# Softmax sums of the first two sequences by TensorE instead of ScalarE's accumulator

## The chip, the core and the metric

The kernel is one program on one core of a Trainium2 chip. It uses five engines that run their own instruction streams and meet at semaphores: TensorE (PE, matrix products), VectorE (DVE), ScalarE (ACT), GpSimd (POOL) and SyncE (SP, which here only issues DMAs). The time is the device time of one execution in microseconds, as the median of several runs. Nothing else of the program's quality is looked at; the question is how many microseconds one execution takes.

## What is computed

The reference is one transformer block with adaptive layer norm, on 16 sequences of 512 tokens of width 128. For every sequence, in float32:

```
h = layernorm(x) * (1 + ca) + sa
q, k, v = h @ wq.T + bq, h @ wk.T + bk, h @ wv.T + bv      # 16 heads of width 8
scores = q k^T / sqrt(8), only |i - j| <= 32 allowed
attn = softmax(scores); x = x + ga * ((attn v) @ wo.T + bo)
h = layernorm(x) * (1 + cb) + sb
top 2 of softmax(h @ gate.T) over 8 experts; the expert input is h times the expert's weight
x = x + gb * (shared expert + the chosen experts), expert = (silu(h w1) * (h w3)) w2
```

The part that the change touches is the softmax: each row of exponentials has to be divided by its sum, before or after the product with v.

## The kernel before

The 16 sequences pass through a software pipeline. While attention runs on sequence b, the experts run on sequence b - 2 and the projections prepare sequence b + 1. Each engine's instructions are written out by hand, for sequences 0 to 4 in a function `fill()`, for 5 to 11 in `body()`, for 12 to 15 in `drain()`; there is one such set per engine, and each engine works strictly in its written order. So what a sequence costs depends on the order in which these calls stand.

Attention goes by 16 steps n per sequence, each of 32 queries for all 16 heads against 96 keys. One step is this chain:

- `scores(b, n)` on PE: four matmuls into one of two halves of the accumulator `ps_s`. It waits until the exponentials of step n - 2 have left that half.
- `maximum(b, n)` on DVE: the row maxima, negated, into `nmx`.
- `probabilities(b, n)` on ACT: four exponentials of 128 x 96 into the ring `p` (4 places), each with its sum taken into `acc` by `accum_out`.
- `turn_p(b, n)` on DVE: the step transposed in blocks of 32 into the ring `pt` (8 places).
- `values(b, kb)` on PE: the products of `pt` with the block-diagonal values `vd` into `ps_O`, for block kb of 32 keys, each group of four heads into its own 32 partitions.

The sums are used in two ways. For sequence 0, `invert_row(n)` on DVE takes reciprocals of the four sums of step n and `scale_row(n)` on POOL multiplies the exponentials by them, ahead of `turn_p(0, n)`; `scale_o(0)` then only copies `ps_O` to `o`. For every later sequence the exponentials stay as they are: `invert_sums(b)` on DVE takes all reciprocals, `turn_sums(b)` on PE transposes them, `copy_sums(b)` on ACT copies them out, `put_sums(b)` on SP writes them to DRAM, `get_sums(b)` on SP reads them back spread over partitions into `rt`, and `scale_o(b)` on DVE multiplies `ps_O` by `rt`. `attn_out(b)` on PE takes `o` from there, `residual(b)` on DVE adds it to x.

Queries and keys travel through DRAM. `high_q`/`high_k` on ACT and `low_q`/`low_k` on DVE split the projections into two parts; SP writes them out (`put_q`, `put_ql`, `put_k`, `put_kl`) and reads them back in the layout for `scores` (`load_q`, `load_k`, for each half of the sequence). `load_q(b, 0)` waits until all of q is in DRAM, `scores(b, 0)` waits until the first half of q and k has landed. The router's weights go the same way (`put_scores`, `get_scores`).

In the fill, experts do not run until sequence 2 has begun, so PE has little to do during sequences 0 and 1. `warm(count)` fills its stream with matmuls whose result nobody reads; they stand in PE's order and take time there like all others.

Of the kernel before, what the change touches and what calls it, by code (L numbers as in the profile page):

```python
# [23 lines left out]
ALU = mybir.AluOpType  # L24
# [5 lines left out]
H, DH = 16, 8  # L30
# [30 lines left out]
def build(nc, x, w13, w2, wqkv, wo, gate, bias, borow, cT, wmod, out):  # L61
    ctx = ExitStack()
    with ctx:
# [32 lines left out]
        bmask = sb("bmask", [128, HJ])  # L96
        mhalf = sb("mhalf", [128, 1])
# [103 lines left out]
        rc_d, nm_d = sem("rc_d"), sem("nm_d")  # L201
# [85 lines left out]
        def _(sp):  # L287
# [146 lines left out]
            def put_sums(b):  # L434

                sp.wait_ge(rst_cp, b)
                if b > 1:
                    sp.wait_ge(r_in, 16 * b - 16)
                for h in range(2):
                    sp.dma_start(r_scr.rearrange("g j (h n) q -> h n g j q", h=2)[h], rst[:, h]).then_inc(r_wr, 16)  # L440

            def get_sums(b):

                sp.wait_ge(r_wr, 32 * b)
                if b > 1:
                    sp.wait_ge(o_d, b)
# [18 lines left out]
            def fill():  # L465
# [26 lines left out]
                load_gb(0)  # L492
# [7 lines left out]
                load_ga(2)  # L500
# [5 lines left out]
                put_sums(1)  # L506
                load_q(2, 1, 0)
                get_sums(1)
                load_k(2, 1, 0)
                load_x(4)  # L510
                load_bias(4)
                put_q(3, 1)
# [7 lines left out]
                get_scores(1, 1)  # L520
                get_scores(1, 2)
                get_scores(1, 3)
                put_sums(2)
                load_q(3, 1, 1)
                get_sums(2)
                load_k(3, 1, 1)
                put_q(4, 0)
                load_bias(5)
                load_ga(3)
                load_x(5)  # L530
                put_ql(4, 0)
                load_gb(1)
# [6 lines left out]
                load_ga(4)  # L539
# [6 lines left out]
                load_k(4, 1, 0)  # L546
                load_bias(6)
                load_gb(2)
                get_scores(2, 3)
                put_q(5, 1)  # L550
                load_x(6)
                put_ql(5, 1)
# [124 lines left out]
        def _(pool):  # L677
# [148 lines left out]
            def scale_row(n):  # L826

                pool.wait_ge(rc_d, n + 1)
                nc.gpsimd.tensor_tensor(p[:, n % PRING], p[:, n % PRING],  # L829
                                        rs[:, n, :].unsqueeze(2).to_broadcast([128, HG, MK]), ALU.mult).then_inc(nm_d, 1)  # L830
# [5 lines left out]
            def fill():  # L836

                clear_q()
                spread_var(1, l1, ln1)
                expand_v(0, 0)  # L840
                expand_v(0, 1)
                inverse(1, l1, ln1)
                shift(1, l1, ln1)
                add_bias(0)
                scale_row(0)
                normal(1, l1, ln1)
                scale_row(1)
                scale_row(2)
                scale_row(3)
                scale_row(4)  # L850
                add_bias(1)
                scale_row(5)
                scale_row(6)
                scale_row(7)
                scale_row(8)
                scale_row(9)
                scale_row(10)
                scale_row(11)
                scale_row(12)
                scale_row(13)  # L860
                scale_row(14)
                scale_row(15)
# [4 lines left out]
                add_bias(2)  # L867
                gate_wo(0)
                gate_wo(1)
# [4 lines left out]
                expand_v(1, 0)  # L874
                expand_v(1, 1)
                scaled_low(0, 0, 0)
                spread_var(3, l1, ln1)
                inverse(3, l1, ln1)
                route_scores(0)
                route_both(0)  # L880
                route_weights(0)
                shift(3, l1, ln1)
                normal(3, l1, ln1)
                add_bias(3)
                expand_v(2, 0)
# [297 lines left out]
        def _(act):  # L1183
# [65 lines left out]
            def copy_sums(b):  # L1249

                act.wait_ge(rst_mm, b)
                if b > 1:
                    act.wait_ge(r_wr, 32 * b - 32)
# [2303 lines left out]
```

## Time and profile before

| | us |
|---|---|
| median of 3 runs | 665.83 (665.41 to 667.18) |
| profiled execution, its own time | 666.87 |
| profiled execution, span from first to last instruction | 664.9 |
| PE busy over the span | 644.2 (97%) |
| DVE busy | 587.4 (88%) |
| POOL busy | 579.5 (87%) |
| ACT busy | 557.4 (84%) |
| mean granted TensorE clock | 0.993 of full speed |

All durations come from the one profiled execution. Busy shares are averages over the whole span; the filler matmuls of `warm` count as busy PE. A row of the timeline gives the start in us from the span's beginning, the duration of the row, engine, line, operation, output and inputs, shapes and a count of merged instructions; in square brackets stands how long the engine was idle before it and what ended that. Matmul ends are modelled, so the distance between two starts is the better measure of what a matmul costs.

### The profile page before, as it was taken

How to read it: one execution, taken by the hardware profiler on the slowest of the kernel's cores; microseconds unless marked ns; L12 is line 12 of the kernel's file. 1: busy time of each engine (PE TensorE's matmuls, PEld its weight loads, DVE VectorE, ACT ScalarE, POOL GpSimd, SP SyncE). 2: the span in 40 equal slices, each digit the busy share in tenths (PEclk: the TensorE clock that was granted, in tenths of full speed). 3: DMA queues.
4: the chain of work that ended last, by engine and by line, in shares of the span. 5: the costliest groups of instructions: out<-in, count | busy, mean ns of one | idle time of the engine just before them, and what ended most of it. 6: DMA issues, size and time to landing. Idle time of an engine off the chain costs nothing. (4 is left out here: it accounts for less than half of the span.)

```text
span 664.9 us, 19607 instructions
## 1 busy us (share of the span) xinstructions
PE 644.2 (97%) x6136; PEld 563.2 (85%) x6136; DVE 587.4 (88%) x1582; ACT 557.4 (84%) x2458; POOL 579.5 (87%) x684
## 2 busy tenths in 40 slices
PE   8899989999999999999999999999999999999997
PEld 6888768888888898989898888888898888888776
DVE  5588868999999999999999999999999999997765
ACT  5598888989898999999898999999898998895442
POOL 7575767999999999999999999999999998888864
PEclk9899999999999999999999999999999999999999
DMA  6787777777877788777888797788778686805041
GB/s 219 194 217 158 211 211 207 207 206 206 240 196 199 191 237 212 209 201 223 221 208 205 184 244 196 206 229 219 204 202 229 176 237 170 238 13 162 3 149 33
DMA packets 194647, 127.51 MB, mean 192 GB/s; under 512 B 110784, under 2 KB 171632, under 8 KB 194416
## 3 DMA queue, kind: packets, MB, share of 16 engines
q1 hardware_dynamic: 194544, 126.27, 70.6%
q8 instruction: 49, 0.80, 0.5%
q14 instruction: 54, 0.44, 0.2%
HBM read 96.10 MB, written 30.14 MB: 190 GB/s over the span
## 5 line engine op out<-in xcount | busy, mean ns | idle before, releaser
L1244 ACT ACTIVATE p<-ps_s,nmx 128x96 f32<-128x96 f32 x1024 | 332.3, 347 | 28.9 <-DVE nmx L1793 27.6
L1244 ACT ACTIVATION_READ_ACCUMULATOR p<-ps_s,nmx 128x1 f32 x1024 | 218.1, 213 | 0.0
L766 POOL TENSOR_TENSOR xs<-h,sbc 128x512 f32<-128x512 f32 x128 | 166.1, 1306 | 5.3 <-DMA sbc<-s_scr 4.1
L772 POOL TENSOR_TENSOR xl<-xs,xh 128x512 fp32r<-128x512 f32 x120 | 154.0, 1285 | 16.4 <-ACT xh L1266 15.5
L2794 PEld LDWEIGHTS ps_s<-k,q 128*128 128x128 f32 x1024 | 139.6, 192 | 22.9 <-ACT p L1244 7.3
L1793 DVE TENSOR_REDUCE nmx<-ps_s 128x4 f32<-128x384 f32 x256 | 136.5, 547 | 25.3 <-PE ps_s L2794 23.4
L2861 PE MATMUL ps_Y<-w2s,g 128*128 128x128 f32 x1152 | 153.6, 279 | 1.3 <-DVE g L1911 1.3
L2861 PEld LDWEIGHTS ps_Y<-w2s,g 128*128 128x128 f32 x1152 | 140.2, 192 | 6.6 <-DVE g L1911 2.1
L2794 PE MATMUL ps_s<-k,q 128*128 128x96 f32 x1024 | 139.9, 269 | 5.6 <-DMA q<-q_scr 2.2
L1820 DVE STREAM_TRANSPOSE pt<-p 128x384 f32<-128x384 f32 x256 | 135.7, 558 | 1.7 <-POOL p L829 0.8
L1902 DVE SCALAR_TENSOR_TENSOR th<-th,ps_A 128x512 f32<-128x512 f32 x136 | 91.9, 676 | 10.1 <-ACT th L1287 8.8
L1266 ACT ACTIVATE xh<-xs 128x512 fp32r<-128x512 f32 x128 | 81.4, 637 | 17.5 <-POOL xs L766 17.3
L1287 ACT ACTIVATE th<-ps_A 128x512 f32<-128x512 f32 x136 | 83.1, 611 | 15.3 <-PE ps_A L2718 14.9
L1911 DVE TENSOR_TENSOR g<-th,ps_B 128x512 f32<-128x512 f32 x136 | 91.7, 674 | 4.5 <-PE ps_Y L2861 1.7
L2716 PE MATMUL ps_A<-xh,w13h 128*128 128x512 f32 x136 | 63.1, 464 | 0.1
L744 POOL TENSOR_TENSOR vd<-vt,bmask 128x1024 f32<-128x1024 f32 x32 | 60.7, 1901 | 2.3 <-DVE vt L1788 2.3
L2716 PE MATMUL ps_B<-xh,w13h 128*128 128x512 f32 x136 | 55.7, 410 | 0.4 <-DVE g L1911 0.3
L2718 PE MATMUL ps_A<-xl,w13h 128*128 128x512 f32 x136 | 54.0, 397 | 0.0
L2718 PE MATMUL ps_B<-xl,w13h 128*128 128x512 f32 x136 | 53.9, 397 | 0.0
L2717 PE MATMUL ps_A<-xh,w13l 128*128 128x512 f32 x136 | 53.7, 395 | 0.0
L2717 PE MATMUL ps_B<-xh,w13l 128*128 128x512 f32 x136 | 53.5, 393 | 0.0
L2817 PE MATMUL ps_O<-pt,vd 128*32 128x96 f32 (+2 forms) x2304 | 52.4, 237 | 0.3 <-POOL vd L744 0.3
(149 smaller groups left out, 1026.4 us busy)
## 6 DMA issues: line engine op xcount, KB each, us to landing
sbc<-s_scr SPq DMA_DIRECT2D x64, 512.0 KB, 6.2
k<-k_scr SPq DMA_DIRECT2D x62, 384.0 KB
q<-q_scr SPq DMA_DIRECT2D x128, 96.0 KB
k<-k_scr SPq DMA_DIRECT2D x31, 336.0 KB
k_scr<-kh SPq DMA_DIRECT2D x32, 256.0 KB, 3.1
q_scr<-qh SPq DMA_DIRECT2D x32, 256.0 KB, 2.9
xr<-x SPq DMA_DIRECT2D x16, 256.0 KB, 4.0
k_scr<-kl SPq DMA_DIRECT2D x16, 256.0 KB, 2.8
```

The costliest lines, as they stand in the source:

```text
L766: nc.gpsimd.tensor_tensor(xs[:, n % 2], h2[:, par], sbc[:, n - 1], ALU.mult).then_inc(xs_d, 1)
L772: nc.gpsimd.tensor_tensor(xl[:, n % XRING], src, xh[:, n % XRING].bitcast(F32), ALU.subtract).then_inc(xl_d, 1)
L1244: last = nc.scalar.activation(p[:, n % PRING, gg, :], ps_s[:, n % 2, MK * gg:MK * gg + MK], ACT.Exp, bias=nmx[:, n, gg:gg + 1], accum_out= ...
L1793: nc.vector.tensor_reduce(nmx[:, n, :], ps_s[:, n % 2, 0:ACC].rearrange("p (g k) -> p g k", g=HG), AX.X, ALU.max, negate=True).then_inc(mx ...
L1820: nc.vector.transpose(pt[:, n % TRING].rearrange("p g r q -> p (g r q)"), p[:, n % PRING].rearrange("p g k -> p (g k)")).then_inc(tr_d, 1)
L1902: nc.vector.scalar_tensor_tensor(th[:, par], th[:, par], 1.0, banks(b, n)[0], ALU.add, ALU.mult).then_inc(v_d, 1)
L1911: nc.vector.tensor_tensor(g[:, par], th[:, par], banks(b, n)[1], ALU.mult).then_inc(g_d, 1)
L2716: mm(dst, wh, xh, start=True, stop=False)
L2717: mm(dst, wl, xh, start=False, stop=False)
L2718: return mm(dst, wh, xl, start=False, stop=True)
L2794: last = mm(ps_s[:, n % 2, MK * gg:MK * gg + MK], heads[:, h, gg, nl], k4[:, h, gg, :, MB * nl:MB * nl + MB], start=gg == 0, stop=gg == HG ...
L2861: last = mm(ps["Y"][:, QB * a:QB * a + QB], g[:, par, QB * a:QB * a + QB], w2s[:, e, :], start=n == 0 and a == 0, stop=n == NX - 1, skip_g ...
```

## The change

For sequences 0 and 1 the sums are made on PE. A constant `ones8` (128 x 32, ones where a partition belongs to a head of the group, zeros elsewhere) is built by POOL. Next to every matmul of `values(b, kb)` with `vd` there is now a second one with the same `pt` operand and `ones8` as weights; it goes into `ps_A` for sequence 0 and into `ps_Y` for sequence 1, which the experts use only later. `scale_o(b)` for these two takes the reciprocal of that accumulator into `rt` (128 x 512) and multiplies. The exponentials of sequences 0 and 1 are issued without `accum_out`. `invert_row` and `scale_row` are gone, and for sequence 1 so are `invert_sums`, `turn_sums`, `copy_sums`, `put_sums` and `get_sums`. The filler matmuls write to `ps_B` instead of `ps_A`; there are 101 of them from `scores(0, 0)` to `scores(2, 0)`, where 121 stood before. The first `down` of sequence 0, which writes `ps_Y`, waits for `scale_o(1)`. And the fill of all five engines is written in another order.

```diff
+            const(nc.gpsimd.memset(ones8[:], 1.0))
+            keep(ones8[:], [[-32, HJ], [0, DH]], 0, 1, val=0.0)
+            keep(ones8[:], [[32, HJ], [0, DH]], 31, -1, val=0.0)
...
                 for gg in range(HG):
-                    last = nc.scalar.activation(p[:, n % PRING, gg, :], ps_s[:, n % 2, MK * gg:MK * gg + MK], ACT.Exp,
-                                                bias=nmx[:, n, gg:gg + 1],
-                                                accum_out=acc[:, par, n, gg:gg + 1])
+                    if b < 2:
+                        last = nc.scalar.activation(p[:, n % PRING, gg, :], ps_s[:, n % 2, MK * gg:MK * gg + MK], ACT.Exp,
+                                                    bias=nmx[:, n, gg:gg + 1])
...
             def turn_p(b, n):
 
-                if seq_is(b, 0):
-                    dve.wait_ge(nm_d, n + 1)
-                else:
-                    dve.wait_ge(exp_d, NMB * b + n + 1)
+                dve.wait_ge(exp_d, NMB * b + n + 1)
...
                 dve.wait_ge(pv_mm, NMB * b + NMB)
-                if seq_is(b, 0):
-                    nc.vector.tensor_copy(o[:], ps["O"][:]).then_inc(o_d, 1)
-                    return
-                dve.wait_ge(r_in, 16 * b)
-                dve.wait_ge(wo_mm, b)
+                if b > 0:
+                    dve.wait_ge(wo_mm, b)
+                if b < 2:
+                    nc.vector.reciprocal(rt[:], ps["AY"[b]][:]).then_inc(rc_d, 1)
+                    dve.wait_ge(rc_d, b + 1)
+                else:
+                    dve.wait_ge(r_in, 16 * b - 16)
                 nc.vector.tensor_tensor(o[:], ps["O"][:], rt[:], ALU.mult).then_inc(o_d, 1)
...
+                        if b < 2:
+                            last = mm(ps["AY"[b]][r, MB * n0:MB * n0 + MB * cnt],
+                                      ones8[:].rearrange("p j d -> p (j d)"),
+                                      src, start=kb == 0 and run is runs[0], stop=kb == NMB - 1, skip_group_check=True)
...
-                if n == 0 and not seq_is(b, 0):
-                    pe.wait_ge(f_d, b)
+                if n == 0:
+                    if seq_is(b, 0):
+                        pe.wait_ge(o_d, 2)
+                    else:
+                        pe.wait_ge(f_d, b)
...
@@ SP, fill @@
                 get_scores(0, 3)
-                put_sums(1)
                 load_q(2, 1, 0)
-                get_sums(1)
                 load_k(2, 1, 0)
```

Three places show how the order moves. First VectorE around `scale_o(0)`, during the steps of sequence 1: `nmx` is `maximum`, `pt` is `turn_p`, `hl`, `ql` and `kl` are the low parts of the next sequence's h, q and k. Before:

```order
70 L1820 STREAM_TRANSPOSE pt<-p 128x384 x2
71 L1793 TENSOR_REDUCE nmx<-ps_s 128x4
72 L1788 STREAM_TRANSPOSE vt<-ps_M 128x512
73 L1827 COPY o<-ps_O 128x512
74 L1793 TENSOR_REDUCE nmx<-ps_s 128x4
75 L1820 STREAM_TRANSPOSE pt<-p 128x384
76 L1760 SCALAR_TENSOR_TENSOR hl<-ps_M,mod,hh 128x512
77 L1793 TENSOR_REDUCE nmx<-ps_s 128x4
78 L1840 TENSOR_TENSOR x<-ps_M,xr 128x512
```

And the same place of the changed kernel (its lines have other numbers):

```order
55 L1792 STREAM_TRANSPOSE pt<-p 128x384 x2
56 L1775 TENSOR_REDUCE nmx<-ps_s 128x4
57 L1801 RECIPROCAL rt<-ps_A 128x512
58 L1805 TENSOR_TENSOR o<-ps_O,rt 128x512
59 L1775 TENSOR_REDUCE nmx<-ps_s 128x4 x2
60 L1742 SCALAR_TENSOR_TENSOR hl<-ps_M,mod,hh 128x512
61 L1814 TENSOR_TENSOR x<-ps_M,xr 128x512
```

The copy of `ps_O` has become a reciprocal and a product; the transpose of v (`vt`) has moved ahead into sequence 0, and one `turn_p` stands behind `residual` now.

Second PE at the end of sequence 0, from its filler on: `ps_s` is `scores`, `ps_A<-wqh` or `ps_B<-wqh` is `warm`, `ps_O` is `values`. Before:

```order
77 L2723 MATMUL ps_A<-wqh 128x384 x8
78 L2794 MATMUL ps_s<-k,q 128x96 x8
79 L2723 MATMUL ps_A<-wqh 128x384 x8
80 L2794 MATMUL ps_s<-k,q 128x96 x4
81 L2723 MATMUL ps_A<-wqh 128x384 x3
82 L2794 MATMUL ps_s<-k,q 128x96 x4
83 L2817 MATMUL ps_O<-pt,vd 32x96 x16
```

And now:

```order
177 L2680 MATMUL ps_B<-wqh 128x384 x11
178 L2751 MATMUL ps_s<-k,q 128x96 x8
179 L2680 MATMUL ps_B<-wqh 128x384 x6
180 L2751 MATMUL ps_s<-k,q 128x96 x4
181 L2680 MATMUL ps_B<-wqh 128x384
182 L2751 MATMUL ps_s<-k,q 128x96 x4
183 L2776 MATMUL ps_O<-pt,vd 32x96
184 L2779 MATMUL ps_A<-pt,ones 32x96
```

The counts of fillers have changed, and products with `vd` and with `ones8` alternate, pair by pair, in the same 32 partitions.

Third SyncE from the router's weights of sequence 0 on: `s_scr` and `sbc` are `put_scores(0)` and `get_scores(0)`, `r_scr` and `rt` the sums, `q` and `k` the second half of sequence 2. Before:

```order
51 L420 DMA s_scr<-smT 32x128
52 L431 DMA sbc<-s_scr 128x1024 x4
53 L440 DMA r_scr<-rst 8x16x32 x2
54 L375 DMA q<-q_scr 24x32x32 x4
55 L447 DMA rt<-r_scr 128x1x512
56 L391 DMA k<-k_scr 96x4x256 x2
57 L391 DMA k<-k_scr 96x4x224
```

And now:

```order
49 L421 DMA s_scr<-smT 32x128
50 L432 DMA sbc<-s_scr 128x1024 x4
51 L376 DMA q<-q_scr 24x32x32 x4
52 L392 DMA k<-k_scr 96x4x256 x2
53 L392 DMA k<-k_scr 96x4x224
```

The three DMAs of the sums of sequence 1 are gone from between the loads.

## Rows read from the trace of the kernel before

**Rows 1.** Busy time by stretch: us, PE, PEld, DVE, ACT, POOL, PEclk, DMA, GB/s

```profile
28.00:56.00 28.00, 27.67 (x252) 24.26 (x253) 20.52 (x60) 23.56 (x132) 18.24 (x25) 0.95 0.82 197
...
200.00:237.00 37.00, 36.79 (x382) 32.69 (x374) 35.04 (x97) 33.96 (x156) 35.58 (x42) 1.00 0.78 206
```

**Rows 2.** Timeline of PE, where sequences 0, 1 and 2 begin

```profile
26.92 1.47 PE L2794 MATMUL ps_s<-k,q 128*128 128x96 f32 x8 [2.20 <-DMA q<-q_scr]
...
53.18 1.68 PE L2723 MATMUL ps_A<-wqh 128*128 128x384 f32 x8
54.70 0.99 PE L2794 MATMUL ps_s<-k,q 128*128 128x96 f32 x8
...
83.32 1.10 PE L2794 MATMUL ps_s<-k,q 128*128 128x96 f32 x8 [0.83 <-DMA k<-k_scr]
```

**Rows 3.** Timeline of SP's DMA issues for sequences 0, 1 and 2

```profile
18.45 1.98 SPq L401 DMA_DIRECT2D k<-k_scr  x3
...
39.39 1.20 SPq L335 DMA_DIRECT2D q_scr<-qh  x2
...
47.24 1.92 SPq L391 DMA_DIRECT2D k<-k_scr  x3
...
67.04 1.20 SPq L335 DMA_DIRECT2D q_scr<-qh  x2
...
75.45 1.93 SPq L391 DMA_DIRECT2D k<-k_scr  x3
```

**Rows 4.** Timeline of ACT: a sum read, the next exponential, later `high_q(2)`

```profile
28.44 0.19 ACT L1244 ACTIVATION_READ_ACCUMULATOR p<-ps_s,nmx 128x1 f32 x1
28.53 0.33 ACT L1244 ACTIVATE p<-ps_s,nmx 128x96 f32<-128x96 f32 x1
...
66.31 0.70 ACT L1227 ACTIVATE qh<-ps_M,bqk 128x512 fp32r<-128x512 f32 x1
```

**Rows 5.** Timeline of POOL: `q4` cleared, `scale_row(0)`, `normal(1)`

```profile
14.09 1.81 POOL L824 MEMSET q<- 96x2048 f32 x1
...
32.75 0.82 POOL L829 TENSOR_TENSOR p<-p,rs 128x384 f32<-128x384 f32 x1
33.56 1.75 POOL L735 TENSOR_SCALAR l_xn<-xr,l_rstd,l_nm 128x128 f32<-128x128 f32 x4
```

**Rows 6.** DVE reciprocals, grouped by form over the whole span

```profile
L1803 DVE RECIPROCAL rs<-acc 128x64 f32<-128x64 f32 x15 | 7.8, 518 | 0.0
...
L1808 DVE RECIPROCAL rs<-acc 128x4 f32<-128x4 f32 x16 | 2.1, 154 | 0.5 <-ACT p L1244 0.5
```

**Rows 7.** Timeline of PE: five key blocks of `values`, then `flip`; later `project_q(2)`

```profile
59.19 0.98 PE L2817 MATMUL ps_O<-pt,vd 128*32 128x96 f32 x40
60.10 0.66 PE L2751 MATMUL ps_M<-ident,l_xn 128*128 128x128 f32 x4
...
65.15 0.39 PE L2718 MATMUL ps_M<-hl,wqh 128*128 128x512 f32 x1
```

**Rows 8.** Timeline of DVE in sequence 1, around `scale_o(0)`

```profile
61.18 0.56 DVE L1793 TENSOR_REDUCE nmx<-ps_s 128x4 f32<-128x384 f32 x1 [0.37 <-PE ps_s L2794]
...
63.80 0.73 DVE L1760 SCALAR_TENSOR_TENSOR hl<-ps_M,mod,hh 128x512 fp32r<-128x512 f32 x1
```

**Rows 9.** Timeline of DVE before and at `scale_o(1)`

```profile
94.89 0.57 DVE L1820 STREAM_TRANSPOSE pt<-p 128x384 f32<-128x384 f32 x1
97.69 0.69 DVE L1831 TENSOR_TENSOR o<-ps_O,rt 128x512 f32<-128x512 f32 x1 [2.23 <-issue]
```

**Rows 10.** Timeline of PE around `attn_out(1)`, and PE's granted clock there

```profile
96.12 0.65 PE L2794 MATMUL ps_s<-k,q 128*128 128x96 f32 x4 [0.29 <-ACT p L1244]
98.48 1.44 PE L2836 MATMUL ps_M<-womg,o 128*128 128x128 f32 x8 [1.71 <-issue]
...
100.57 0.63 PE L2718 MATMUL ps_A<-xl,w13h 128*128 128x512 f32 x1
100.99 0.63 PE L2716 MATMUL ps_B<-xh,w13h 128*128 128x512 f32 x1
...
100.00:102.00 2.00, 2.00 (x6) 1.52 (x6) 2.00 (x8) 1.47 (x7) 0.65 (x1) 0.50 0.90 182
```

More of the change, by code:

```diff
@@ L96, in build @@
         bmask = sb("bmask", [128, HJ])
+        ones8 = sb("ones8", [128, HJ, DH])
         mhalf = sb("mhalf", [128, 1])
@@ L2041, in fill @@
                 maximum(1, 4)
[L2042 removed]
                 scale_o(0)
                 maximum(1, 5)
[L2045 removed]
+                maximum(1, 6)
                 low_h1(2)
[L2047 removed]
                 residual(0, 0)
                 statistics(0, l2, ln2)
+                turn_p(1, 3)
+                low_q(2)
+                moments(0, l2, ln2)
                 maximum(1, 7)
[L2051 to L2052 removed]
                 maximum(1, 8)
                 turn_p(1, 4)
+                low_k(2)
                 turn_p(1, 5)
[L2056 removed]
                 maximum(1, 9)
@@ L2083, in fill @@
                 maximum(2, 0)
-                invert_sums(1, 1)
+                maximum(2, 1)
+                turn_p(1, 15)
                 turn_v(2)
-                maximum(2, 1)
                 maximum(2, 2)
-                turn_p(1, 15)
                 turn_p(2, 0)
@@ L2235, in fill @@
                 low_h1(5)
+                maximum(4, 5)
                 half_silu(2, 0, 0)
-                maximum(4, 5)
+                scale_o(3)
                 combine(2, 0, 0)
+                finish(1)
                 maximum(4, 6)
-                finish(1)
-                scale_o(3)
                 half_silu(2, 1, 1)
@@ L2247, in fill @@
                 statistics(3, l2, ln2)
-                turn_p(4, 5)
-                moments(3, l2, ln2)
-                maximum(4, 8)
-                half_silu(2, 2, 0)
-                maximum(4, 9)
-                combine(2, 2, 0)
+                maximum(4, 8)
+                maximum(4, 9)
+                moments(3, l2, ln2)
+                half_silu(2, 2, 0)
+                combine(2, 2, 0)
+                turn_p(4, 5)
                 low_k(5)
@@ L2978, in fill @@
                 values(1, 2)
+                values(1, 3)
                 router(0, 0)
-                values(1, 3)
                 values(1, 4)
+                scores(1, 12)
+                scores(1, 13)
+                warm(6)
+                scores(1, 14)
+                warm(1)
+                scores(1, 15)
+                warm(4)
+                router_t(0)
                 values(1, 5)
@@ L3005, in fill @@
                 values(1, 10)
+                scores(2, 1)
+                warm(5)
+                scores(2, 2)
+                flip(3, l1, ln1, "M1")
                 values(1, 11)
@@ L3008, in fill @@
                 values(1, 13)
-                warm(2)
+                scores(2, 3)
+                warm(3)
+                scores(2, 4)
+                expert(0, 0)
+                scores(2, 5)
+                project_q(3)
                 values(1, 14)
                 values(1, 15)
-                scores(2, 3)
-                scores(2, 4)
-                expert(0, 0)
-                project_q(3)
-                scores(2, 5)
+                expert(0, 1)
                 scores(2, 6)
-                expert(0, 1)
                 scores(2, 7)
@@ L3154, in fill @@
                 values(4, 5)
+                scores(4, 11)
                 router(3, 1)
```

328 lines of the change are left out of this document (136 added, 192 removed).

## The prediction

> **What bounds the kernel now.** I read the busy time by stretch first, then the timelines of the engines in the fill, then the waits inside it. The table by stretch separates two regimes. A steady sequence takes 37.0 us and PE is busy for 36.79 of them; DVE, ACT and POOL stay 1.4 to 3 us under it. In the fill PE is busy too (27.67 us of 28), but largely with filler [rows 1]. The change does nothing to the steady regime, so it can only move the moment at which that regime begins. I therefore ask for the three moments at which attention on sequences 0, 1 and 2 starts: 26.92, 54.70 and 83.32 [rows 2].
>
> What ends the wait at each? At 26.92 and 83.32 PE was idle and a DMA of q or k released it. At 54.70 PE shows no idle time, only filler, which can hide the same gate. The issues tell: k is issued over 47.24 to 49.16 and scores begin 5.5 us after; k is issued over 75.45 to 77.38 and scores begin 5.9 us after [rows 2, 3]. That is the same distance, so I take the gate to be the landing of q and k in both cases. From the first write of q to the first scores it is 54.70 - 39.39 = 15.3 us for sequence 1 and 83.32 - 67.04 = 16.3 us for sequence 2. This round trip does not shrink with fewer ACT instructions. Only the moment at which q is written can move, and everything on ACT and POOL that does not lead to it is cover.
>
> **Part by part.** Exponentials: 128 of them lose the reading of the accumulator. The read of the sum starts at 28.44 and the next exponential at 28.53, 0.09 us behind it [rows 4]; that distance is what each read adds. 4 x 0.09 = 0.36 us per step, 32 steps, 11.5 us of ACT in all. Bounds: nothing (the read overlaps entirely) to 0.19 per exponential (its whole duration), so 0 to 0.76 per step. I take the distance between the starts. Little of it is on the path, since two more steps of the chain (scores, maximum) and the round trip cover it.
>
> POOL: sixteen `scale_row` of 0.82 us go, 13 us. Their cover is POOL's idle time, but one is on the path: `scale_row(0)` at 32.75 stood ahead of `normal(1)` at 33.56 [rows 5]. h, q and k of sequence 1 hang on that. It gives 0.8 us. Sixteen `invert_row` of 0.154 on DVE [rows 6] and the shorter steps give another 0.4, with `low_h1(1)` reached sooner. So q of sequence 1 is written 1.2 us earlier and scores(1, 0) stands at 53.5. Bounds 0.4 to 2.0: either `scale_row` alone counts by half, or DVE gains what the reciprocals and 2 x 0.36 of ACT allow. In the new order eleven fillers stand before scores(1, 0), 11 x 0.19 = 2.1 us by the eight that took 53.18 to 54.70 [rows 2], where eight stood; they end about when the data land.
>
> The constant `ones8` puts three more POOL instructions, of 128 x 32 each, ahead of the clearing of `q4` at 14.09. The clearing itself, 96 x 2048, ends at 15.90, and the first load that needs it is issued at 18.45 [rows 3, 5]. The three would have to take 2.5 us to be felt, more than the whole clearing of 1.81. Zero; if that cover were gone, each us on them would be one on everything.
>
> Sums on PE: 40 records, twenty matmuls, took 59.19 to 60.10, that is 0.0455 us each and 0.18 per key block of four [rows 7]. The second matmul of each pair doubles it: 144 matmuls x 0.0455 = 6.6 us over both sequences, of which sixteen plus eight blocks (4.9 us) lie in the fill, against 20 fillers x 0.19 = 3.8 us taken out. There PE waits for data anyway. The last eight blocks (1.5 us) lie after 83.32 and partly under PE's own wait of 1.71 us [rows 10]. I charge 0.3. Bounds 0 (all in that wait) and 6.3 (rival B).
>
> Reciprocals on DVE, the term against the change. There is no 128 x 512 reciprocal in the trace. The forms there are take 154 ns for 4 columns and 518 for 64 [rows 6], which is 364 / 60 = 6.1 ns per column. 512 columns: 0.15 + 508 x 0.0061 = 3.2 us. Bounds: 3.0 without any fixed part, and 4.1 = 8 x 0.518 if the fixed part comes again with each 64. I take 3.2. The Trainium skill (VectorE: DVE Perf Modes, First, the fixed hardware budget) says that a reciprocal is a hardware division with a repeat count of 8; if this means 8 cycles of its 0.96 GHz per column, 64 columns cost 533 ns and 512 cost 4.3 us. Of this the trace shows 518 ns for 64 with all overhead in it, so it does not bear out a full 8 cycles; by the rule the sum would be 2 x 1.1 = 2.2 us worse, 667.1.
>
> On the path in sequence 1: from maximum(1, 4) to the end of `low_h1(2)` it was 64.53 - 61.18 = 3.35 us [rows 8]. Now it is 0.5 (maximum) + 3.2 + 0.7 (product, by the one at 97.69 [rows 9]) + 1.0 (two maxima) + 0.7 = 6.1: 2.75 later. Against it stand the 1.2 of the earlier start and 1.1 by which maximum(1, 4) comes sooner after it (three shorter steps, `turn_v` out of the way). `hl` is 0.45 late. But q had waited: the last product of project_q(2) began at 65.15 and was over at 65.54, `high_q(2)` ran at 66.31 behind two steps of ACT [rows 4, 7]. That is 0.77 of cover. So q of sequence 2 is written 0.3 earlier, scores(2, 0) at 83.0: the fill of sequence 1 gives back 0.9 of the 1.2.
>
> In sequence 2, before, DVE was through with its other work at 95.46, stood 2.23 us for the sums' round trip and multiplied at 97.69; attn_out(1) followed at 98.48 [rows 9, 10]. That wait goes, with `invert_sums(1)` (0.5). What is late next is the reciprocal itself. When does DVE reach it? At the latest at 95.46 less the 0.3 of the earlier start and less what no longer stands ahead, one maximum (0.5), one transpose (0.5) and the small reciprocals (0.5): 93.7. At the earliest without any wait: from 83.0 it is 0.6 to the first maximum, then six maxima, five transposes, `vt`, `hl`, one `th` and one `g`, 11 x 0.5 + 4 x 0.65 = 8.1, so 91.7. I take 93.2, near the late end, since today's waits for PE in this stretch come back. o is ready 3.2 + 0.7 + 0.1 later, at 97.2, and attn_out(1) starts at 97.3, 1.2 us earlier than now, 0.9 more than the 0.3 at the start; off it go 0.3 for the extra matmuls. Queued behind the reciprocal are half_silu(0, 1) and maximum(2, 6); the exponential of that step has the expert's input ahead of it on ACT in both orders, and this covers them.
>
> Sum: 0 + (-1.2) + 0.9 + (-0.9) + 0.3 = -0.9 us, on the profiled execution's 666.87 (span 664.9), so 666.0. The runs shown have a median 1.04 us below that execution: 665.83 - 0.9 = 664.9. Later stages are PE-bound and carry the shift; the reordering of sequences 2 to 4 I cost at nothing, with PE at its 37 us as cover, +-1.
>
> **Rivals.** A, faster: the reciprocal is hidden and the clock holds. After the gap ahead of 98.48 PE's granted clock is 0.50, its 1.2 GHz level, and equal 512-column products start 0.42 apart, at full clock half of it [rows 10]. From 98.48 to 102 all work runs at half rate, 3.5 us for 1.8: 1.7 us lost. If the gap is shorter and the clock stays at 2.4 GHz, and sequence 1 keeps its whole 1.2, the sum is -0.9 - 0.9 - 1.7 = -3.5: 662.3. For it: two waits vanish. Against: my own arrival of the reciprocal still leaves PE 2 us idle before attn_out(1).
>
> B, slower: pairs do not overlap. Today four matmuls in four different groups of 32 partitions run side by side; eight passes take 0.18 us per key block, so one set of four passes takes 0.09. Now two neighbours share a group. If the second holds up the next group, the sixteen passes of a block run one by one, 16 x 0.09 = 1.4 instead of 0.36, 1.0 more per block. The eight blocks after 83.32 then cost 8 us, less the 1.7 of wait: 6.3, of which 0.3 is counted, so 6.0 more, 670.9. It decides from about 0.6 us per block on, where the wait is used up. For it: the order shows the pairs; against: the passes of one group already queue behind each other without holding the others.
>
> C, no gain: the reciprocal costs 4.1. Both are on the path, 2 x 0.9 = 1.8 more: 666.7, and if the four maxima and transposes behind it cannot catch up before `hl`, another 1 us, 667.7.
>
> That nothing happens (gates entirely set by DMA traffic) gives 665.8 and lies inside the forecast's own range.
>
> **How the numbers follow.** Forecast 0.42, with a range of its own of 663.0 to 666.8; A 0.29; B 0.12; C 0.17. A measurement here tells about 0.3%, 2.0 us, from no change: 663.8 and 667.8 are the borders. Faster: A and 0.08 of the forecast, 0.37. Slower: B and half of C, 0.20. Same: the rest, 0.43. For 8 in 10 the range goes from 660.5 (A with 2.0 instead of 1.2 at the first gate and DVE 1.0 sooner at `scale_o(1)`) to 668.8 (C and the 1 us of the reordering), which leaves out B and a tail of A.
>
> **What would show it.** Right: scores(1, 0) at 53 to 54 and scores(2, 0) at 82.5 to 83.5, with q and k released by DMA there; reciprocals of 3.0 to 3.4 us; a key block of pairs in 0.36 us; attn_out(1) near 97 behind `scale_o`. Wrong: scores(2, 0) earlier than 82 (the round trip was not the gate, or the reciprocal is off the path), a block above 0.6 us, a reciprocal of 4 us, or no drop of the clock near 100.

## The result and the profile after

| | before | after |
|---|---|---|
| median of 7 runs, us | 666.23 (665.30 to 668.69) | 670.59 (669.19 to 673.12) |
| profiled execution, span | 664.9 | 668.9 |
| scores(0, 0) / scores(1, 0) | 26.92 / 54.70 | 26.28 / 55.30 |
| scores(2, 0) | 83.32 | 85.90 |
| scores(3, 0) / scores(4, 0) | 121.3 / 158.8 | 123.7 / 161.2 |

The changed kernel is slower: the ratio is 1.0069, 95% interval 1.0052 to 1.0086, about 4.6 us (the two medians are 4.4 apart). Forecast were 664.9 us and a range of 660.5 to 668.8; the time lies above both.

By stretch (us, PE, PEld, DVE, ACT, POOL, PEclk, DMA, GB/s), against [rows 1]:

```profile
28.00:56.00 28.00, 26.93 (x361) 22.00 (x360) 17.80 (x42) 17.73 (x66) 6.57 (x10) 1.00 0.78 188
200.00:237.00 37.00, 36.80 (x372) 32.68 (x371) 35.09 (x97) 33.88 (x154) 35.37 (x42) 1.00 0.79 210
```

The steady stretch is the same. In the fill ACT has lost 5.8 us of 23.6 and POOL 11.7 of 18.2, DVE 2.7. PE, the engine that carries the gate, is nearly as full as before, 26.93 for 27.67. So three engines were relieved, and the time is longer all the same.

The timeline of PE, against [rows 2, 7, 10]. The first rows are the gate of sequence 0; those from 47.59 the steps and key blocks ahead of scores(1, 0); those from 59.06 two regular blocks; then the third product of project_q(2), scores(2, 0), and attn_out(1):

```profile
26.28 1.09 PE L2751 MATMUL ps_s<-k,q 128*128 128x96 f32 x8 [1.01 <-DMA q<-q_scr]
...
47.59 0.65 PE L2751 MATMUL ps_s<-k,q 128*128 128x96 f32 x4
48.16 0.39 PE L2776 MATMUL ps_O<-pt,vd 128*32 128x96 f32 x8
48.35 0.37 PE L2779 MATMUL ps_A<-pt,ones 128*32 128x96 f32 x8
48.52 0.28 PE L2776 MATMUL ps_O<-pt,vd 128*32 128x64 f32 x2
...
51.09 0.44 PE L2680 MATMUL ps_B<-wqh 128*128 128x384 f32 x1
...
53.30 2.17 PE L2680 MATMUL ps_B<-wqh 128*128 128x384 f32 x11
55.30 0.99 PE L2751 MATMUL ps_s<-k,q 128*128 128x96 f32 x8
...
59.06 0.39 PE L2776 MATMUL ps_O<-pt,vd 128*32 128x96 f32 x8
...
59.42 0.39 PE L2776 MATMUL ps_O<-pt,vd 128*32 128x96 f32 x8
...
67.99 0.40 PE L2675 MATMUL ps_M<-hl,wqh 128*128 128x512 f32 x1
...
85.90 0.54 PE L2751 MATMUL ps_s<-k,q 128*128 128x96 f32 x4
...
100.74 1.13 PE L2799 MATMUL ps_M<-womg,o 128*128 128x128 f32 x8 [1.63 <-issue]
```

A regular block takes 59.42 - 59.06 = 0.36 us, as worked out. But the five blocks 6 to 10 take 51.09 - 48.16 = 2.93 us, 0.59 each. And ahead of 55.30 there is no wait in the row, and the last load of q or k for it had landed at 52.9: the eleven fillers end there, not the data.

SP's issues, against [rows 3]: first q, then k of sequence 1, then q and k of sequence 2.

```profile
37.39 1.20 SPq L336 DMA_DIRECT2D q_scr<-qh  x2
...
45.69 1.92 SPq L392 DMA_DIRECT2D k<-k_scr  x3
...
69.14 1.20 SPq L336 DMA_DIRECT2D q_scr<-qh  x2
...
77.73 1.93 SPq L392 DMA_DIRECT2D k<-k_scr  x3
```

q of sequence 1 is written 2.0 us earlier than before, at 37.39 for 39.39, and k is issued 1.55 earlier; scores(1, 0) is 0.6 later all the same. q of sequence 2 is written 2.1 later, and scores(2, 0) begins 2.58 later.

The timeline of DVE, against [rows 8, 9]:

```profile
61.22 0.56 DVE L1775 TENSOR_REDUCE nmx<-ps_s 128x4 f32<-128x384 f32 x1 [0.54 <-PE ps_s L2751]
61.69 3.35 DVE L1801 RECIPROCAL rt<-ps_A 128x512 f32<-128x512 f32 x1
65.07 0.69 DVE L1805 TENSOR_TENSOR o<-ps_O,rt 128x512 f32<-128x512 f32 x1
65.68 1.01 DVE L1775 TENSOR_REDUCE nmx<-ps_s 128x4 f32<-128x384 f32 x2
66.61 0.74 DVE L1742 SCALAR_TENSOR_TENSOR hl<-ps_M,mod,hh 128x512 fp32r<-128x512 f32 x1
...
95.80 0.67 DVE L1885 TENSOR_TENSOR g<-th,ps_B 128x512 f32<-128x512 f32 x1
96.56 3.36 DVE L1801 RECIPROCAL rt<-ps_Y 128x512 f32<-128x512 f32 x1
99.95 0.69 DVE L1805 TENSOR_TENSOR o<-ps_O,rt 128x512 f32<-128x512 f32 x1
```

maximum(1, 4) is where it was (61.18 before), the reciprocal takes 3.35, and `low_h1(2)` starts 2.81 later. project_q(2) waits for it; PEld is the loading of weights on PE:

```profile
67.40 0.19 PEld L2673 LDWEIGHTS ps_M<-hh,wqh 128*128 128x128 f32 x1 [0.38 <-DVE hl L1742]
```

ACT, POOL and the reciprocals by form, against [rows 4 to 6]: a step of exponentials without sums, the clearing of `q4`, `normal(1)`, and all forms of the reciprocal (the last figures are busy us, mean ns of one, idle time before them).

```profile
29.92 1.03 ACT L1224 ACTIVATE p<-ps_s,nmx 128x96 f32<-128x96 f32 x4 [0.41 <-DVE nmx L1775]
```

```profile
15.06 1.80 POOL L825 MEMSET q<- 96x2048 f32 x1
...
31.86 1.74 POOL L733 TENSOR_SCALAR l_xn<-xr,l_rstd,l_nm 128x128 f32<-128x128 f32 x4
```

```profile
L1783 DVE RECIPROCAL rs<-acc 128x64 f32<-128x64 f32 x14 | 7.3, 518 | 0.0
L1801 DVE RECIPROCAL rt<-ps_Y 128x512 f32<-128x512 f32 x1 | 3.4, 3358 | 0.1
L1801 DVE RECIPROCAL rt<-ps_A 128x512 f32<-128x512 f32 x1 | 3.3, 3347 | 0.0
```

Four exponentials take 1.03 us, `normal(1)` starts 1.70 earlier with `scale_row(0)` gone, and the clearing is 0.97 later.

### The profile page after: what moved, and what is told of

The parts are those of the page before. It is cut to its first block and busy times, and to the rows that moved or that the text cites. A ratio compares the mean times of both kernels' runs of the same rounds, so it can differ in the third digit from the quotient of the medians.

```text
span 668.9 us, 19976 instructions
## 1 busy us (share of the span) xinstructions
PE 649.3 (97%) x6402; PEld 565.9 (85%) x6402; DVE 590.8 (88%) x1567; ACT 546.5 (82%) x2329; POOL 569.0 (85%) x671
## 5 line engine op out<-in xcount | busy, mean ns | idle before, releaser
L1227 ACT ACTIVATE p<-ps_s,nmx 128x96 f32<-128x96 f32 x896 | 290.1, 347 | 19.0 <-DVE nmx L1775 18.3
L1227 ACT ACTIVATION_READ_ACCUMULATOR p<-ps_s,nmx 128x1 f32 x896 | 192.2, 215 | 0.0
L2776 PE MATMUL ps_O<-pt,vd 128*32 128x96 f32 (+2 forms) x2304 | 59.2, 238 | 0.0
```

The source lines that it names most:

```text
L1227: last = nc.scalar.activation(p[:, n % PRING, gg, :], ps_s[:, n % 2, MK * gg:MK * gg + MK], ACT.Exp, bias=nmx[:, n, gg:gg + 1], accum_out= ...
```

## The experiments

All times are medians with the lowest and highest run; a ratio is against the kernel before, measured alongside on the same chip, with its 95% interval. "After" is the changed kernel, and a distance from it is the difference of the ratios (1.0069 for after) times 666 us. Two ratios whose intervals overlap widely are not told apart by the times; the traces then carry the reading. Moments come from one profiled execution each. In those of kernels that are alike up to there, scores(0, 0) began anywhere from 25.8 to 27.1, so a difference of moments below 1 us is read from scores(0, 0) on.

**1. `old_order`: the new mechanism in the old order of the fill.** The five lists of `fill()` are those of the kernel before, less the calls that no longer exist.

```diff
 # fill() of every engine: before's order, without
-scale_row, invert_row, invert_sums(1), turn_sums(1), copy_sums(1), put_sums(1), get_sums(1)
```

> The changed kernel with the order of the fill of before on all five engines: the sums of sequences 0 and 1 by pairs of matmuls, their exponentials without sums, two reciprocals of 128x512, but every call where it stood before (121 fillers, v of sequence 1 transposed behind maximum(1, 4), put and get of the sums of sequence 1 left out). Theory M (the mechanism costs: the reciprocal stands on the path from sequence 1's start to its q and k, the pairs lengthen PE's stream): at least as slow as the changed kernel, 670 to 673 us, with scores(2, 0) at 86 or later. Theory O (the new order costs, the mechanism is neutral): within 1.5 us of before, 665 to 668, with scores(2, 0) near 83.

Measured 680.38 (679.48 to 683.81), ratio 1.0229 (1.0201 to 1.0258). scores(1, 0) stands at 54.2, scores(2, 0) at 89.1, scores(3, 0) at 131.3. In the old order the mechanism costs about 15 us and the new order gives 10.7 of it back. PE is idle for 2.92 us ahead of attn_out(0) there, where the changed kernel has fillers, and for 2.76 ahead of attn_out(1), where it waits 1.63. Its profiled execution has a granted clock of 0.88 from 56 to 84, where the changed kernel has 1.00, so part of these moments is clock.

**2. `copy_rt`: both 128x512 reciprocals replaced by copies.** The division is left out.

```diff
-nc.vector.reciprocal(rt[:], ps["AY"[b]][:]).then_inc(rc_d, 1)
+nc.vector.tensor_copy(rt[:], ps["AY"[b]][:]).then_inc(rc_d, 1)
```

> The changed kernel with each of the two 128x512 reciprocals (3.35 us in its profile) replaced by a copy of the same accumulator (about 0.65 us); the division is left out. Theory R (both reciprocals are on the path, 2.7 us each): q of sequence 2 is written 2.0 to 2.7 us earlier, scores(2, 0) at 83 to 84 instead of 85.9, attn_out(1) another 1 to 2.7 earlier, total 4 to 5 us less, 665.5 to 666.8. Rival P (PE's own stream in sequences 0 and 1 sets the pace): at most 1.5 us less, 669 to 670.6.

Measured 669.61 (668.48 to 674.43), ratio 1.0066 (1.0038 to 1.0094): 0.2 us under after, less than the interval can tell from nothing. Its DVE rows show why:

```profile
62.42 0.68 DVE L1801 COPY rt<-ps_A 128x512 f32<-128x512 f32 x1
63.13 0.69 DVE L1805 TENSOR_TENSOR o<-ps_O,rt 128x512 f32<-128x512 f32 x1
...
65.31 0.74 DVE L1742 SCALAR_TENSOR_TENSOR hl<-ps_M,mod,hh 128x512 fp32r<-128x512 f32 x1
67.60 0.69 DVE L1814 TENSOR_TENSOR x<-ps_M,xr 128x512 f32<-128x512 f32 x1 [1.55 <-PE ps_M L2799]
```

and PE in the same kernel:

```profile
64.63 1.97 PE L2680 MATMUL ps_B<-wqh 128*128 128x384 f32 x10
66.44 1.05 PE L2799 MATMUL ps_M<-womg,o 128*128 128x128 f32 x8
...
67.69 0.40 PE L2673 MATMUL ps_M<-hh,wqh 128*128 128x512 f32 x1
```

`o` is ready at 63.8 and `hl` at 66.05, but PE comes to attn_out(0) at 66.44 and to project_q(2) at 67.69, from its own stream. From the first of the ten fillers ahead of attn_out(0) to project_q(2) it is 3.06 us (64.63 to 67.69), for 3.50 in the changed kernel (63.91 to 67.41): 0.4 us is what the reciprocal had held PE back. Two paths end there within 1 us of each other: DVE's with the reciprocal, and PE's with pairs and fillers. Taking away one shows the other. And what was won was lost behind it. Counted from scores(0, 0), which began at 27.01 for 26.28, q of sequence 2 was written 0.6 sooner, but scores(2, 0), at 87.16 with 0.74 of waiting for k, came 0.5 later: from the write of q to it 17.9 us passed, for 16.8.

**3. `fill11`: 3 instead of 11 fillers ahead of scores(1, 0).**

```diff
                 scores(0, 15)
-                warm(11)
+                warm(3)
```

> The changed kernel with 3 instead of 11 fillers between scores(0, 15) and scores(1, 0), 8 x 0.18 = 1.4 us less in PE's stream at a place where q and k had landed at 52.9 and scores(1, 0) began at 55.3. Theory P (PE's own stream holds the start of sequence 1): scores(1, 0) 1.4 us earlier, and all behind it, total 1.0 to 1.5 us less, 669.1 to 669.6. Rival R (the path from there is DVE's, and the clock falls for want of filler): within 0.5 us of the changed kernel, or slower by up to 1.5 with a granted clock below 1.00 near 54.

Measured 672.08 (671.03 to 674.02), ratio 1.0090 (1.0065 to 1.0115), no gain. scores(1, 0) did come 1.7 us earlier (53.6), 1.4 of it counted from scores(0, 0), which is the eight fillers; so the fillers had held it. The gain was lost by scores(2, 0), at 86.5 with 0.92 us of waiting for k. First attn_out(0), which stands ahead of project_q(2), waited:

```profile
65.51 1.16 PE L2799 MATMUL ps_M<-womg,o 128*128 128x128 f32 x8 [0.67 <-POOL womg L716]
```

`o` was ready at 64.70, with the reciprocal; `womg`, which `gate_wo(0)` on POOL makes, at 65.45. So a third path ends here, POOL's. q was written only 0.67 earlier, and the last of its three writes landed at 74.17, where 74.22 stood in the changed kernel. The median above after's is not explained by this stretch: from scores(3, 0) to sequence 8 the profiled execution stands where the changed kernel's stood. It loses 3.6 us behind the start of the last sequence, where its granted clock is 0.89 from 600 to 630, for 1.00.

**4. `no_pairs`: without the second matmuls.** One 128x512 matmul of other data fills the accumulator per sequence; the sums are left out.

```diff
-                        if b < 2:
-                            last = mm(ps["AY"[b]][r, ...], ones8[:]..., src, ...)
+                if b < 2 and kb == 0:
+                    last = mm(ps["AY"[b]][:], wqh[:, 0, :], hh[:], start=True, stop=True)
```

> The changed kernel without the second matmul of each pair: the sums are left out, and one 128x512 matmul of other data per sequence fills the accumulator that the reciprocal reads. Theory P (the pairs, above all in the blocks split by the ring, cost more than their 0.18 us per block and hold scores(0, 15) and the start of sequence 1): scores(1, 0) 1.5 to 2.5 us earlier, total 2 to 4 us less, 666.6 to 668.6. Rival R: pairs lie under waits, total 0 to 1.5 us less, 669.1 to 670.6.

Measured 667.44 (664.97 to 672.01), ratio 1.0015 (0.9993 to 1.0038), 3.6 us under after, and the two intervals lie apart. scores(1, 0) 53.4, scores(2, 0) 84.1; counted from scores(0, 0) (27.08) they are 2.7 and 2.6 sooner. Of the costs that were measured by taking something out, the pairs are the largest. The execution that was profiled, at 671.99 one of the slowest, gives part of it back: after PE had been idle for 1.84 of the 4 us from 80 to 84, its clock was lower.

```profile
84.00:88.00 4.00, 3.90 (x45) 3.60 (x46) 1.99 (x4) 2.24 (x13) 1.08 (x2) 0.65 0.67 169
88.00:92.00 4.00, 4.00 (x38) 3.39 (x38) 1.71 (x4) 2.54 (x13) 3.14 (x2) 0.50 1.02 361
```

0.50 is the 1.2 GHz level; the same stretch of the changed kernel is at 1.00.

**5. `with_acc`: accum_out back on the exponentials of sequences 0 and 1,** its sums unused.

```diff
-                    if b < 2:
+                    if b < 0:
                         last = nc.scalar.activation(p[...], ps_s[...], ACT.Exp, bias=nmx[...])
```

> The changed kernel with accum_out back on the exponentials of sequences 0 and 1 (the sums are taken and not used). If the reading of the sums is hidden in the fill (PE's order, the pairs and the fillers set the pace, theory P): a step of exponentials takes 1.3 us instead of 1.05, the starts of scores(1,0) and scores(2,0) move by less than 0.7, time within 1 us of the changed kernel's 670.6. If ACT is on the path of each step (theory A: the exponentials without sums are what the change lives on): 0.3 us for each of about 26 steps between 26.3 and 85.9, so 5 to 8 us slower, 676 to 678.

Measured 675.74 (673.43 to 677.87), ratio 1.0156 (1.0130 to 1.0181): 5.8 us over after, intervals apart. A step of four exponentials takes 1.40 us with its reads instead of 1.05; scores(1, 0) stands at 58.0 and scores(2, 0) at 90.9, 2.7 and 5.0 later. The first of these is in part clock (0.76 from 49 to 56); the other 2.3 arise at a clock of 1.00. The sum reads are on the path in this order. What the change takes from ACT is worth 5 to 6 us, and it is spent.

**6. `grouped`: the same products, ordered by weights instead of by partition group.** First all with `vd`, the four groups in turn, then all with `ones8`; where the columns of a block run over the ring's end, the two runs of columns are the next outer loop.

```diff
-                for gg in range(HG):
-                    for run in runs:
-                        mm(ps["O"]..., vd...)
-                        if b < 2: mm(ps["AY"[b]]..., ones8...)
+                for ones in range(2 if b < 2 else 1):
+                    for run in runs:
+                        for gg in range(HG):
+                            mm(dst..., ones8 if ones else vd..., ...)
```

> The changed kernel with each key block's products in another order: first all with vd (four groups of 32 partitions in turn), then all with ones8, instead of pair by pair in one group. If neighbours in the same 32 partitions hold each other up (the blocks 7, 8 and 11 to 13 of sequence 0 at 0.5 to 0.6 us), a block takes 0.33 to 0.36 everywhere, some 2 us of PE are saved in each sequence and the time falls by 1 to 2 us, to 669. If a block is sixteen passes at the same rate whatever the order, nothing moves: 670.6 within 0.7.

Measured 668.40 (665.81 to 671.44), ratio 1.0037 (1.0015 to 1.0058), 2.1 us off after, where the intervals just overlap. The same five blocks on PE:

```profile
48.03 0.37 PE L2779 MATMUL ps_O<-pt,vd 128*32 128x96 f32 x8
...
48.39 0.36 PE L2779 MATMUL ps_O<-pt,vd 128*32 128x64 f32 x16
48.56 0.36 PE L2779 MATMUL ps_A<-pt,ones 128*32 128x64 f32 x16
48.73 0.36 PE L2779 MATMUL ps_O<-pt,vd 128*32 128x32 f32 x16
...
49.86 0.45 PE L2680 MATMUL ps_B<-wqh 128*128 128x384 f32 x1
```

They take 49.86 - 48.03 = 1.83 us for 2.93, with as many matmuls of the same shapes. scores(1, 0) is at 54.0, scores(2, 0) at 84.1, scores(3, 0) at 120.8. scores(3, 0) comes sooner than before the change (121.3), and still the median is above it. The five slowest of twelve executions (670.1 to 671.4) have a mean granted clock of 0.988 to 0.993, the other seven (up to 668.8) 0.994 to 1.000. So part of the distance may be clock, but the kernel before has an execution at 0.989 that takes 666.6, and no run separates it.

**7. `lean`: 18 fillers out of the stretch before project_q(2).**

```diff
-warm(11) ... warm(10) attn_out(0) warm(2) project_q(2)
+warm(3)  ... warm(2)  attn_out(0)         project_q(2)
```

> The changed kernel with 3 fillers instead of 11 ahead of scores(1,0), 2 instead of 10 ahead of attn_out(0) and none instead of 2 behind it: 18 fillers, 3.4 us of PE, out of the stretch before project_q(2). Theory P (PE's order holds project_q(2) back): scores(1,0) at 53.6, project_q(2) begins by 66.1, q written at 67.3 to 67.6 instead of 69.1, scores(2,0) near 84.3, time 1.5 us down, 669. Theory R (the reciprocal holds low_h1(2) at 65.6 whatever PE does): the gain at project_q(2) stops at 0.9, scores(2,0) at 85.0 to 86, 670. Theory D (the round trip of q and k waits in the DMA queues, as with 3 fillers alone, where q was written 0.7 earlier and landed no earlier): scores(2,0) at 86.5, 671 to 672.

Measured 670.41 (669.41 to 671.89), ratio 1.0069 (1.0048 to 1.0090): nothing. Its profiled execution had a clock of 0.88 from 28 to 56 and scores(1, 0) at 55.3, so the moments can't be compared; the distance from there to scores(2, 0) is 31.8, for 30.6. PE now waits ahead of attn_out(0):

```profile
67.17 1.16 PE L2799 MATMUL ps_M<-womg,o 128*128 128x128 f32 x8 [2.00 <-POOL womg L716]
```

Again it is POOL's `womg` (67.12) that ended last, 0.67 behind `o` (66.45). But `hl` was ready only at 68.04, and project_q(2) began at 68.09. So the time fits R, and it would fit POOL's path as well; this run doesn't tell them apart. `gate_wo(0)` was never moved by itself. It stands earlier in `grouped_lean` and in the two kernels built on it, and there it ends 5 to 6.5 us ahead of attn_out(0).

**8. `hl_first`: q taken from behind the reciprocal, and still fewer fillers.**

```diff
 # DVE
-maximum(1, 4) scale_o(0) maximum(1, 5) maximum(1, 6) low_h1(2) residual(0, 0) ... low_q(2)
+maximum(1, 4) low_h1(2) scale_o(0) maximum(1, 5) low_q(2) maximum(1, 6) residual(0, 0) ...
 # PE: project_q(2) ahead of scores(1, 6) and attn_out(0); 18 fillers fewer than fill11
 # ACT: high_q(2) ahead of probabilities(1, 5); SP: put_q(2, 0) ahead of two loads
```

> As the kernel before this one, and the reciprocal taken off the path to q: low_h1(2) stands ahead of scale_o(0) on VectorE, project_q(2) ahead of attn_out(0) on PE, high_q(2) one step earlier on ACT, the write of q ahead of two loads on SP; 9 fillers fewer in the rest of sequence 1. If reciprocal and fillers together set the gate of sequence 2: q written at 63 to 64, its low part at 67, k at 70, scores(2,0) at 81 to 82 instead of 85.9, and time 3 to 4.5 us down, 666 to 667.5, no better than the kernel before the change or just so. If the expert input or the steps of sequence 1 take the place as what ends last: scores(2,0) at 84 or later and 669 to 670. A gap on PE before 81 could let the clock fall: then 1.5 to 3 us come on top.

Measured 673.69 (670.38 to 677.86), ratio 1.0128 (1.0090 to 1.0167), worse. q of sequence 2 was written at 63.9, 5.2 us earlier, and q and k had landed at 83.4 for 85.6. But scores(2, 0) began at 86.3: maximum(1, 5) still stands behind the reciprocal (65.59), so the steps of sequence 1 end as late as before; attn_out(0) waited 1.46 for `womg` as well. And the clock was lower: 0.85 from 78 to 82, where PE with fewer fillers was busy for 3.28 of 4 us, and 0.72 from 82 to 86, for 1.00 in the changed kernel. How much each of the two cost was not separated. Of six executions the three slowest (676.1 to 677.9) have mean clocks of 0.979 to 0.983.

**9. `grouped_copy`: grouped products and copies.** The division is left out. Edit as in 2 and 6.

> The kernel with grouped products (668.4) and copies instead of the two reciprocals; the division is left out. With the pairs as they were the copies gave 1.0 (theory P: PE's order was the later of the two paths). If with PE's path 2.9 shorter the reciprocal is the later one (at scale_o(0) and low_h1(2), and again ahead of attn_out(1), where PE was idle 1.57 us), the copies give 2 to 3 us now: 665.4 to 666.4. If the reciprocals never set the end: 668.4 within 0.7.

Measured 666.96 (664.99 to 669.96), ratio 1.0011 (0.9987 to 1.0035), 1.7 us under grouped where the copies alone had given 0.2. That is what is expected if the reciprocal counts once PE's path is shorter, but the intervals overlap, and these times don't show it. The trace of experiment 10 and the time of 11 bear it out.

**10. `grouped_lean`: `grouped`, 10 fillers fewer around attn_out(0), gate_wo(0) earlier on POOL.**

```diff
-scores(1, 6) warm(10) attn_out(0) warm(2) project_q(2)
+scores(1, 6) warm(2)  attn_out(0)         project_q(2)
```

> Grouped products, 10 fillers fewer around attn_out(0) and gate_wo(0) ahead of add_bias(2) on POOL; the reciprocals stay. o(0) is ready at 64.4 in the grouped kernel and attn_out(0) began at 64.5, so the fillers end just when the reciprocal does: theory R says nothing is gained, 668.4 within 0.7. If PE's order still holds project_q(2) back: 0.4 to 1 us, 667.4 to 668.

Measured 668.17 (666.54 to 671.93), ratio 1.0028 (1.0006 to 1.0050): within 0.6 us of grouped, as R says. In its trace PE is idle for 1.38 us ahead of attn_out(0), until `o` is ready at 67.36; `womg` had been ready since 60.99. Here the reciprocal alone is what PE waits for.

**11. `early_rt`: `grouped_lean`, and the reciprocals in parts.** A query's sum is final once the next key block is through, so each part is taken in a gap between blocks, and PE waits for it before the next one.

```diff
+            def invert(b, lo, hi, done):
+                dve.wait_ge(pv_mm, NMB * b + done)
+                nc.vector.reciprocal(rt[:, MB * lo:MB * hi], ps["AY"[b]][:, MB * lo:MB * hi]).then_inc(rc_d, 1)
...
+ invert(0, 0, 5, 6) ... invert(0, 5, 9, 13) ... invert(0, 9, 12, 13) ... maximum(1, 4) invert(0, 12, 16, 16) scale_o(0)
+ invert(1, 0, 4, 8) maximum(2, 0) invert(1, 4, 8, 11) ... invert(1, 8, 16, 16) scale_o(1)
```

> As the kernel before this one, and the reciprocals taken in parts as soon as their columns are final, in gaps between the key blocks (PE waits for them before the next block): four parts for sequence 0 (160, 128, 96 and 128 columns), three for sequence 1 (128, 128, 256). At scale_o(0) only 128 columns are left (0.93 us instead of 3.35), at scale_o(1) 256 (1.7). Theory R: scale_o(0) 2 us earlier, q of sequence 2 written 1 to 1.5 us earlier, scores(2,0) near 83, attn_out(1) near 96, time 1.5 to 3 us under the grouped kernel, 665.5 to 667, as fast as the kernel before the change or faster. If the parts only move the wait into the steps (maximum later, values waiting for DVE): 668 to 669.

Measured 666.34 (664.20 to 670.23), ratio 0.9999 (0.9977 to 1.0021): the 4.6 us are repaired, and this interval lies apart from after's. Cutting the reciprocals is worth 1.9 us of it by the ratios: ten of its twelve executions lie at or below 666.54, where `grouped_lean` has one of twelve. DVE in it:

```profile
46.13 1.15 DVE L1800 RECIPROCAL rt<-ps_A 128x160 f32<-128x160 f32 x1
...
60.74 0.95 DVE L1800 RECIPROCAL rt<-ps_A 128x128 f32<-128x128 f32 x1
61.79 0.69 DVE L1811 TENSOR_TENSOR o<-ps_O,rt 128x512 f32<-128x512 f32 x1
...
93.70 1.76 DVE L1800 RECIPROCAL rt<-ps_Y 128x256 f32<-128x256 f32 x1
95.59 0.69 DVE L1811 TENSOR_TENSOR o<-ps_O,rt 128x512 f32<-128x512 f32 x1
```

and PE at attn_out(1), which no longer waits (nor does the clock fall: 1.00 from 96 to 106):

```profile
95.39 0.99 PE L2764 MATMUL ps_s<-k,q 128*128 128x96 f32 x8
96.38 1.13 PE L2813 MATMUL ps_M<-womg,o 128*128 128x128 f32 x8
```

**12. `early_fill`: `early_rt` with 6 instead of 11 fillers ahead of scores(1, 0).** Edit as in 3.

> As the kernel before this one, and 6 instead of 11 fillers ahead of scores(1,0). q and k land at 52.9 and scores(1,0) began at 54.0 in the grouped kernel: it can begin at 53.1. If the gate of sequence 2 follows it: 0.9 off, 665 to 666. If it does not, as with 3 fillers in the changed kernel (scores(1,0) 1.7 earlier, nothing kept): the same time as without.

Measured 667.74 (664.45 to 671.97), ratio 1.0022 (0.9997 to 1.0048). Its profiled execution has scores(1, 0) at 53.0, scores(2, 0) at 82.2 and scores(3, 0) at 119.1, 1.1 to 1.2 us ahead of `early_rt` throughout. Its median is 1.4 higher all the same, and the intervals overlap; whether the missing fillers cost clock in more executions stays open.

## Why the prediction was wrong

**The step that failed** is the charge for the pairs: "There PE waits for data anyway", and with it the eleven fillers that "end about when the data land". The 0.36 us of a regular block was right. But five of the blocks ahead of scores(1, 0) took 2.93 us, not 1.8, and I booked all of them against removed fillers without adding up PE's stream. q and k of sequence 1 landed at 52.9, 1.5 earlier than before; PE came to scores(1, 0) at 55.30. I had taken PE's filler as free time, and by then it was the path. The runs put the pairs at 3.6 us in all (no_pairs), some 2.1 of them from the order within a block (grouped), for the 0.3 that I charged. Rival B had the right term and sign, but neither the mechanism nor the place: a regular block of pairs takes 0.36 as forecast, the five average 0.59, not 1.4, and the loss arises ahead of scores(1, 0), while B had it behind 83.32. Only a block that the ring's end splits passes B's 0.6: the one that starts at 48.52 takes about 1.0. That B's 670.9 lies beside the measured 670.59 is luck.

**The exponentials** were mis-sized the other way. The distance between the starts (0.09 us each) was right, a step takes 1.05 us for 1.40; but "little of it is on the path" was wrong. The experiment with the sums put back costs 5.8 us. So a second error, of opposite sign, stands in the sum of -0.9.

**The first gate and q of sequence 1**: q was written 2.0 earlier, at the upper bound of my 0.4 to 2.0. But 0.64 of that is an earlier scores(0, 0), no more than it scatters by. Counted from there it is 1.36, and my 1.2 was about right. No cost of POOL's constants shows, as costed, though the clearing starts 0.97 later.

**The reciprocal** of 3.2 measured 3.35 and 3.36, inside 3.0 to 4.1. Rival C falls. The Trainium skill (VectorE: DVE Perf Modes, First, the fixed hardware budget) gives a repeat count of 8; read as 8 cycles per column, that is an estimate of 4.3 us, and the trace does not agree.

**The path of sequence 1**: from maximum(1, 4) to the end of `low_h1(2)` it is 67.35 - 61.22 = 6.13 us, forecast 6.1; the term "2.75 later" came out as 2.78. What was to stand against it did not come: the earlier start (1.2) was 0.6 late instead, and maximum(1, 4) came 0.56 sooner after scores(1, 0), not 1.1. So q of sequence 2 was 2.1 late instead of 0.3 early. The round trip behind it, which I had taken as fixed, took 16.8 us for 16.3, and scores(2, 0) is at 85.90, not 83.0. The miss of 2.9 is thus 1.8 from the start of sequence 1, 0.5 from its steps and 0.5 from the round trip. Here the largest part of the loss sits, 2.6 us by then. The round trip is no constant: from the write of q to scores(2, 0) 16.3 us passed in `grouped`, 17.9 in `copy_rt` and 18.1 in `fill11`. Why, no run shows.

**The stretch to attn_out(1)** was sized rightly: DVE reached the reciprocal 96.56 - 85.90 = 10.7 us after scores(2, 0), forecast 10.2, and PE waited 1.63 for 1.71. Counted from scores(2, 0), attn_out(1) came 0.3 sooner than before, not 0.9. The clock did drop near 100 (0.50 from 102 to 104), as said. But the same wait does not always bring it: with 1.57 us of idle time in `grouped`, 1.64 in `fill11` and 1.63 in `with_acc` at that place the clock stayed at 1.00, and in `lean`, with 1.63, it fell to 0.50. `early_rt` has what Rival A needed, no wait and no drop, and takes 666.34, not 662.3.

**The reordering of sequences 2 to 4 at nothing** held in the profiled executions: from scores(2, 0) to scores(4, 0) it is 75.33 us, for 75.51 before. What I had no term for is what the new order of the whole fill is worth to the mechanism, 10.7 us (`old_order`). Without it the kernel would stand at 680. The upper end of the range, 668.8, is 668.7 by its own terms.

**What doesn't add up.** ACT's part gives 5.8 us; the pairs cost 3.6, and the reciprocals 0.2 to 1.9. By these numbers alone the change would be no loss. Each was measured by taking one thing out of a path on which several engines end close together, so they are no terms of a sum, and what the other 5 to 7 us are stays open.

Of the 4.6 us the profiled execution shows 2.4 to 2.7 from scores(3, 0) to sequence 8. Another 1.4 arise at sequences 9 and 10, where DVE waits for the load of `rt` (1.34 us at 361.77, 0.89 at 399.27). `fill11` and `copy_rt`, which share these stages, add 0.3 and nothing there, so I take it for a matter of that one execution. How much of the median comes from such waits and from the clock in the fill was not separated.

## What to carry over

Filler on an engine hides its slack only as long as the data are later than the filler: before charging new work on such an engine at nothing, add up its written stream to the gate and compare it with the landing. Where paths end within 1 us of each other, taking away one term alone measures almost nothing: 0.2 us for the reciprocals by themselves, and 1.9 once the pairs were grouped and `gate_wo(0)` was out of the way. Test such terms together, and read at every wait who released it: in `fill11` and `lean` it was a third engine. A long operation on a strictly ordered engine should be cut into parts that become ready early and fit its idle time.

## What the runs showed of the hardware

- Matmuls into 32-partition groups are sensitive to order at equal count and shape. Alternating two weights in one group, with the columns in two runs, the five blocks took 2.93 us; with the four groups in turn, 1.83. Regular blocks cost 0.33 to 0.36 in both orders, so the loss sits in the blocks that are split (about 1.0 and 0.6 us) and the two right behind them (0.48 each). Why those two, no run shows.
- Reciprocals on DVE: 0.72 us for 96 columns, 0.93 to 0.95 for 128, 1.15 for 160, 1.76 for 256, 3.35 for 512: a fixed 0.1 and 6.3 ns per column (2.63 us over the 416 columns between the first and the last).
- The clock was lower after PE had had less to do: 0.72 from 82 to 86 in `hl_first`, which has fewer fillers, and 0.50 from 88 to 92 in `no_pairs`, which has fewer matmuls; the changed kernel stands at 1.00 in both. It is not the same in every execution: a wait of 1.6 us ahead of attn_out(1) was followed by 0.50 in `after` and `lean` and by 1.00 in `fill11`, `with_acc` and `grouped`.
